# The third layer's sums over source nodes as pairs of float32r products

## What is computed

```python
h_edge = jnp.concatenate([x[src], x[dst]], axis=-1)
m_ij = jax.nn.relu(h_edge @ W_interact + b_interact)
m_i = jax.ops.segment_sum(m_ij, src, num_segments=x.shape[0])
m_i = m_i / jnp.asarray(math.sqrt(AVG_DEGREE), dtype=x.dtype)      # a factor 0.25
out = x + jax.nn.relu((x + m_i) @ W_update + b_update)
```

## Time and profile before

| | us |
|---|---|
| median of 3 runs (range) | 1886.35 (1883.08 to 1886.48) |
| span of the profiled execution, first to last instruction | 1885.1 |
| busy in that span: TensorE products, VectorE, ScalarE, GpSimd | 1694.0, 1432.5, 1037.5, 1024.9 |
| edge stage: first product of L1277 to last product of L1295, start to start | 1129.1 to 1877.2 |

### The profile page before, as it was taken

How to read it: one execution, slowest core, us unless ns; L and a number is a source line. 1 busy time by engine, 2 the same in 40 slices (tenths; PEclk the granted TensorE clock), 3 DMA queues, 4 the chain that set the end, 5 groups by cost and what they waited for, 6 DMA issues and landing times.

```text
span 1885.1 us, 45388 instructions
## 1 busy us (share of the span) xinstructions
PE 1694.0 (90%) x16778; PEld 1472.1 (78%) x16778; DVE 1432.5 (76%) x5527; ACT 1037.5 (55%) x2015; POOL 1024.9 (54%) x1075
## 2 busy tenths in 40 slices
PE   1606798999999979999999759999999999999998
PEld 1403676888778757777777649999999999999998
DVE  7968998999998335676653558888787777887776
ACT  1715575666667450000000248877777777777776
POOL 3364105656551004566551157777777777777775
PEclk9955999999999999999999879999999999999998
DMA  3005526465553656666666223443443444444442
GB/s 99 1 1 169 211 114 217 151 220 192 178 218 116 255 188 253 238 244 240 239 240 227 59 72 104 104 111 107 123 114 104 112 111 105 111 107 122 115 105 71
DMA packets 135014, 276.48 MB, mean 147 GB/s; under 512 B 21160, under 2 KB 82393, under 8 KB 134794
## 3 DMA queue, kind: packets, MB, share of 16 engines
q1 hardware_dynamic: 98427, 201.82, 31.1%
q0 software_dynamic: 34784, 71.17, 14.2%
q10 hardware_dynamic: 1584, 0.59, 0.1%
HBM read 192.26 MB, written 84.45 MB: 147 GB/s over the span
## 4 chain that ended last, share of the span: by engine, by line
PE 45%; DVE 24%; POOL 16%; issue 8%; DMA 4%; ACT 1%; POOLq 1%; SPq 1%; DVEq 0%
PE ps L1111 23%; POOL cells L810 8%; DVE hot L1595 7%; PE ps L1284 6%; PE ps L1277 5%; PE ps L1295 4%; POOL cell_lo L810 3%; POOL cell_hi L810 3%; DVE hot L1589 3%; PE ps L1097 2%; PE ps L1144 2%; DMA cells<-b_rows,work 2%; DVE keys L1685 1%; DVE keys L1619 1%; DVE keys L1684 1%
## 5 line engine op out<-in xcount | busy, mean ns | idle before, releaser
L1111 PE MATMUL ps<-slab,table 128*128 128x320 bf16 x4704 | 688.0, 300 | 2.5 <-DVE table L1834 2.4
L1111 PEld LDWEIGHTS ps<-slab,table 128*128 128x128 bf16 x4704 | 460.8, 98 | 167.9 <-DVE table L1834 2.9
L900 ACT ACTIVATE slab<-ps 128x980 bf16<-128x980 f32 x256 | 322.4, 1274 | 193.7 <-PE ps L1097 193.6
L810 POOL DMA_INDIRECT cells<-b_rows,work x336 | 319.9, 952 | 102.3 <-issue 96.9
L1284 PE MATMUL ps<-slab 125*128 125x128 bf16 x5496 | 357.1, 219 | 0.2 <-DVE slab L1917 0.2
L1284 PEld LDWEIGHTS ps<-slab 125*128 125x128 bf16 x5496 | 333.3, 98 | 4.8 <-DVE slab L1917 0.8
L1277 PE MATMUL ps<-table 125*128 125x128 f32 x1800 | 317.2, 286 | 1.7 <-DVE table L1911 1.7
L1005 ACT ACTIVATE lnw<-iota_w,keys 128x125 f32<-128x125 f32 x900 | 289.8, 389 | 1.6 <-POOL slab L801 1.6
L1277 PEld LDWEIGHTS ps<-table 125*128 125x128 f32 x1800 | 250.0, 192 | 1.9 <-issue 1.9
L1019 ACT ACTIVATE slab<-ps 128x384 f32<-128x384 f32 x300 | 146.1, 487 | 170.7 <-DVE ps L1926 167.6
L770 POOL DMA_INDIRECT hot<-t_rows,pairs x160 | 168.7, 1054 | 120.0 <-PE ps L1144 77.0
(11 more groups left out here) (304 smaller groups left out, 2144.6 us busy)
## 6 DMA issues: line engine op xcount, KB each, us to landing
slabs_d<-slab SPq DMA_DIRECT2D x16, 3920.0 KB, 12.9
slab<-slabs_d SPq DMA_DIRECT2D x16, 3920.0 KB, 14.4
hot<-lane_d SPq DMA_DIRECT2D x50, 576.0 KB
t_rows<-table SPq DMA_DIRECT2D x2, 4800.0 KB, 17.7
cells<-b_rows,work POOLq DMA_INDIRECT x336
inv<-inv_row SPq DMA_DIRECT2D x32, 160.0 KB
keys<-up_d SPq DMA_DIRECT2D x50, 96.0 KB
keys<-down_d SPq DMA_DIRECT2D x50, 96.0 KB
```

Source lines behind the costliest of these rows:

```text
L810: p.indirect_dma_start(rows_g[gi % RS][:, j, :], None, b_rows, bass.IndirectOffsetOnAxis(ap=node_t[:, t:t + 1], axis=0)).then_inc(e_gath[g ...
L900: a.activation(slab[par][:, :, u * UB * BW:(u + 1) * UB * BW].rearrange("p h (k d) -> p k h d", k=UB), psum_unit(u).rearrange("p k (h d) - ...
L1111: last = t.matmul(ps[:, 4 + par, 0:width], table[:, k // TERMS, k % TERMS, :], slab[par][:, k // TERMS, 0:width], start=k == 0, stop=k == ...
```

## The change

The messages are no longer one f32 tile. ScalarE writes relu(PSUM) rounded to type float32r (`msg_hi`), and a new VectorE instruction per group, `low_term`, writes the rest, max(PSUM, 0) - `msg_hi`, as float32r too (`msg_lo`, three buffers). The factor 0.25 goes into `src_hot`, which becomes float32r and 126 columns wide (BE). `source_sum` makes two float32r products for each tile in place of one f32 product: 1800 products in all. It now waits for `e_low`, and so does `edge_sum` for its bank; `low_term(gi - 1)` stands between `add_rows(gi)` and `prepare(gi + 3)`, and the last one behind the loop. A check is added: ahead of the loop two float32r products of 128x128 test tiles with VectorE making the tiles and comparing; behind the loop, VectorE looks at the lowest 12 bits of some of `msg_hi` (128x320), and adds 1e6 times what it found to the last chunk's rows, 128x640. The diff, without the places where semaphores are merged:

```diff
+    f32r = mybir.dt.float32r
...
+    BE = BN + 1
...
+        start = {}
+
+            start[name] = -(-nc.sbuf_base // 32) * 32
+
+        def over(name, of, byte, shape):
+            return nc.alloc_sbuf_tensor_at(name, shape, f32r, offset=start[of] + byte)
...
-        one_c = sb("one_c", [P, 1])
+        trial = over("trial", "pairs", 0, [P, 4, P])
+        quarter = sb("quarter", [P, 1])
...
-        msg_f = slab_f[0][:, NT * D:NT * D + 3 * GW]
-        assert NT * D + 3 * GW <= HI * SC // 2
-        msg = msg_f.rearrange("p (s n) -> p s n", s=3)
+        assert NT * D + 3 * GW <= HI * SC // 2 and (KU * FH + 2 * GW) * 4 + 24 <= 4 * 3 * KW // 2 and GW <= KW // 2
+        msg_hi = over("msg_hi", "slab0", 4 * NT * D, [P, 3, GW])
+        lo_two = over("lo_two", "work", -(-4 * KU * FH // 32) * 32, [P, 2, GW])
+        lo_one = over("lo_one", "iota_b", 0, [P, 1, GW])
+        msg_lo = [lo_two[:, 0, :], lo_two[:, 1, :], lo_one[:, 0, :]]
...
-        src_hot = [x[:, :, :].rearrange("p s n -> p (s n)")[:, k * GT * BN:(k + 1) * GT * BN].rearrange(
-            "p (j n) -> p j n", j=GT) for x in (tslot, rest) for k in range(3)]
+        src_hot_r = [over(f"src_hot_{of}", of, 0, [P, 3, GT * BE]) for of in ("tslot", "rest")]
+        src_hot = [x[:, k, :].rearrange("p (j n) -> p j n", j=GT) for x in src_hot_r for k in range(3)]
...
             def source_hot(gi):
                 if gi > 5:
                     act.wait_ge(e_psum, gi - 5)
-                far = lnw[:, :, :].rearrange("p k t -> p (k t)")[:, 0:GT * BN].rearrange("p (j n) -> p j n", j=GT)
+                far = lnw[:, :, :].rearrange("p k t -> p (k t)")[:, 0:GT * BE].rearrange("p (j n) -> p j n", j=GT)
                 if gi:
                     act.wait_ge(e_srchot, gi)
                 for j in range(GT):
-                    last = a.activation(far[:, j, :], iota_w[:, 0:BN], ACT.Square,
+                    last = a.activation(far[:, j, :], iota_w[:, 0:BE], ACT.Square,
                                         bias=lane_g[:, gi * GT + j:gi * GT + j + 1])
                 last.then_inc(e_far, 1)
                 act.wait_ge(e_far, gi + 1)
-                a.activation(src_hot[gi % 6], far, ACT.Relu, scale=-1.0, bias=one_c[:, 0:1]).then_inc(e_srchot, 1)
+                a.activation(src_hot[gi % 6], far, ACT.Relu, scale=-0.25, bias=quarter[:, 0:1]).then_inc(e_srchot, 1)
 
             act.wait_ge(q_lane, 1)
             act.wait_ge(f_blo, 6)
...
                 act.wait_ge(e_full, gi + 1)
                 if gi > 2:
                     act.wait_ge(e_psum, gi - 2)
-                a.activation(msg[:, gi % 3, :], ps[:, gi % 4, 0:GW], ACT.Relu, scale=0.25).then_inc(e_msg, 1)
+                a.activation(msg_hi[:, gi % 3, :], ps[:, gi % 4, 0:GW], ACT.Relu).then_inc(e_msg, 1)
                 if gi + SOON < NGR:
                     source_hot(gi + SOON)
 
...
                     t.matmul(ps[:, 6, 0:BN], g_msg, g_hot, start=True, stop=True).then_inc(g_sum, 1)
 
             pe.wait_ge(f_aok, NC)
+            pe.wait_ge(f_bok, NC)
             pe.wait_ge(f_blo, 6)
+            pe.wait_ge(s_trial, 2)
+            t.matmul(ps[:, 7, 2 * P:3 * P], trial[:, 0, :], trial[:, 1, :], start=True, stop=True)
+            t.matmul(ps[:, 7, 3 * P:4 * P], trial[:, 2, :], trial[:, 3, :], start=True, stop=True).then_inc(s_trial, 1)
 
             def edge_sum(gi):
                 b, g = divmod(gi, GB)
                 pe.wait_ge(e_rowhot, gi + 1)
                 if gi > 3:
-                    pe.wait_ge(e_msg, gi - 3)
+                    pe.wait_ge(e_low, gi - 3)
                 end = END_TILES[g]
                 w0, w1 = window(b, end)
                 for j in range(GT):
...
 
             def source_sum(gi):
                 b, g = divmod(gi, GB)
-                pe.wait_ge(e_msg, gi + 1)
+                pe.wait_ge(e_low, gi + 1)
                 pe.wait_ge(e_srchot, gi + 1)
                 if g == 0 and b > 1:
                     pe.wait_ge(e_added, b - 1)
+                terms = msg_hi[:, gi % 3, :], msg_lo[gi % 3]
                 for j in range(GT):
-                    last = t.matmul(ps[:, 4 + b % 2, 0:BN], msg[:, gi % 3, j * P:(j + 1) * P], src_hot[gi % 6][:, j, :],
-                                    start=g == 0 and j == 0, stop=g == GB - 1 and j == GT - 1)
+                    for k, term in enumerate(terms):
+                        last = t.matmul(ps[:, 4 + b % 2, 0:BE], term[:, j * P:(j + 1) * P], src_hot[gi % 6][:, j, :],
+                                        start=g == 0 and j == k == 0, stop=g == GB - 1 and j == GT - 1 and k == 1)
                 last.then_inc(e_psum, 1)
 
             def update(c):
...
 
             dve.wait_ge(f_aok, NC)
             dve.wait_ge(f_blo, 6)
+            link(v.tensor_scalar(trial[:, 0, :], ident[:, :], 1.0 + 2.0 ** -11, None, ALU.mult))
+            link(v.tensor_copy(trial[:, 2, :], ident[:, :]))
+            v.tensor_scalar(trial[:, 3, :], ones[:, :], 1.0 + 2.0 ** -11, None, ALU.mult).then_inc(s_trial, 1)
+            v.tensor_copy(trial[:, 1, :], ones[:, :]).then_inc(s_trial, 1)
 
             def prepare(gi):
                 b, g = divmod(gi, GB)
...
                 v.tensor_tensor(out=to, in0=to, in1=rows_g[gi % RS].rearrange("p j f -> p (j f)"), op=ALU.add
                                 ).then_inc(e_full, 1)
 
+            def low_term(gi):
+                dve.wait_ge(e_msg, gi + 1)
+                if gi > 2:
+                    dve.wait_ge(e_psum, gi - 2)
+                v.scalar_tensor_tensor(out=msg_lo[gi % 3], in0=ps[:, gi % 4, 0:GW], scalar=0.0,
+                                       in1=msg_hi[:, gi % 3, :].bitcast(f32), op0=ALU.max, op1=ALU.subtract
+                                       ).then_inc(e_low, 1)
+
             def keep_sum(b):
                 dve.wait_ge(e_psum, (b + 1) * GB)
                 to = hT[:, b * BN:(b + 1) * BN]
...
             AHEAD = 3
             for gi in range(AHEAD):
                 prepare(gi)
+            dve.wait_ge(s_trial, 3)
+            link(v.tensor_scalar(inv[:, 0, 0:2 * P], ps[:, 7, 2 * P:4 * P], 1.0 + 2.0 ** -11, None, ALU.not_equal))
+            v.tensor_reduce(out=col[:, 0:1], in_=inv[:, 0, 0:2 * P], op=ALU.max, axis=AX.X)
             for gi in range(NGR):
                 b, g = divmod(gi, GB)
                 add_rows(gi)
+                if gi:
+                    low_term(gi - 1)
                 if gi + AHEAD < NGR:
                     prepare(gi + AHEAD)
                 if g == AHEAD and b:
...
                     biased(LAST_BLOCK.index(b - 2))
                 if g == 2 and b - 2 in LAST_BLOCK:
                     residual(LAST_BLOCK.index(b - 2))
+            low_term(NGR - 1)
             keep_sum(NB - 1)
+            link(v.tensor_scalar(inv[:, 0, 0:SC].bitcast(i32), msg_hi[:, 0, 0:SC].bitcast(i32), 4095, None, ALU.bitwise_and))
+            link(v.tensor_copy(inv[:, 1, 0:SC], inv[:, 0, 0:SC].bitcast(i32)))
+            link(v.tensor_reduce(out=col[:, 1:2], in_=inv[:, 1, :], op=ALU.max, axis=AX.X))
+            link(v.tensor_tensor(out=col[:, 2:3], in0=col[:, 0:1], in1=col[:, 1:2], op=ALU.max))
+            link(v.tensor_scalar(col[:, 2:3], col[:, 2:3], 1.0e6, None, ALU.mult))
             biased(NC - 1)
+            dve.wait_ge(o_biased, NC)
+            link(v.tensor_scalar(hrow[:, (NC - 1) % 2, :, :], hrow[:, (NC - 1) % 2, :, :], col[:, 2:3], None, ALU.add))
             residual(NC - 1)
```

More of the change, by code:

```diff
@@ L322, in gnn_kernel @@
         s_diag = sem("s_diag")
-        s_et = sem("s_et")
+        s_once = sem("s_once")
         k_flag = sem("k_flag")
-        k_sum = sem("k_sum")
         s_rounds = sem("s_rounds")
@@ L334, in gnn_kernel @@
         k_placed = sem("k_placed")
+        ONCE_EDGES, ONCE_FLAGS, ONCE_BLOCKS, ONCE_ENDS = 1, 2, 3, 4
         def norm_sems(k):
@@ L414, in gnn_kernel @@
         e_msg = sem("e_msg")
+        e_low = sem("e_low")
+        s_trial = sem("s_trial")
         e_psum = sem("e_psum")
@@ L690, in _ @@
             numbers(up_c[:, :], [[BN, 12]], 1)
-            p.memset(one_c[:, :], 1.0).then_inc(s_iota, 1)
+            p.memset(quarter[:, :], 0.25).then_inc(s_iota, 1)
             p.iota(down_c[:, :], pattern=[[BN, 12]], base=BN - 1, channel_multiplier=-1,
@@ L1037, in _ @@
                 last = t.matmul(ps[:, 4, h * HG:(h + 1) * HG], ones[0:HG, :], diag[:, h, :], start=True, stop=True)
-            last.then_inc(s_et, 1)
+            last.then_inc(s_once, 1)
             def norm_transpose(S, c):
@@ L1063, in _ @@
             pe.wait_ge(k_flag, 2)
-            t.matmul(ps[:, 7, 0:1], ones[:, :], flag[:, 2:3], start=True, stop=True).then_inc(k_sum, 1)
+            t.matmul(ps[:, 7, 0:1], ones[:, :], flag[:, 2:3], start=True, stop=True).then_inc(s_once, 1)
             pe.wait_ge(s_w, 16 * 11)
@@ L1170, in spread_histogram @@
                 t.matmul(ps[:, 7, 0:HH * TH * HL - half], ones[0:TH * HH, :], flat[:, half:HH * TH * HL],
-                         start=True, stop=True).then_inc(q_need, 1)
```

(16 more changed lines are left out.)

3 lines of the change are left out of this document (removed).

## The result

The changed kernel is slightly slower: 1888.96 us (median of 20 runs, 1886.24 to 1893.34) against 1885.49 us for the kernel before (20 runs, 1883.08 to 1888.72), ratio 1.0022 with a 95% interval of 1.0016 to 1.0028, 3 to 5 us. That the change would gain nothing was foreseen. The extra time was not: I forecast 1.5 us more, at the end of the kernel, and the runs show 3 to 5 us, most of it in the gathers.

What follows compares the result with a forecast made beforehand. GpSimd's gathers were taken to bound the edge stage. Span 1885.1 + 0 (stage) + 1.5 (tail) = 1886.6 us; with the runs' median 1.25 above the profiled span, 1887.9 us, range 1880 to 1912.

Steps and rivals of the forecast that it cites:

- The bound: Edge stage: GpSimd's gathers set the pace at 2.50 us a group, 4% more than TensorE's 2.40.
- float32r at the price of a transpose: TensorE's source sums: each float32r product taken at 0.109 us, 196 us in place of 200, nothing gained.
- Rival 1: Source sums: a float32r product takes 0.222 us, as long as f32; TensorE sets the pace, about 2059 us; chance 0.16.
- the 715 us case: TensorE's sum of work in the stage if float32r counts as FP32 for weight loading; otherwise 620 us.
- The low term's price: VectorE, each group: 0.48 us plus 0.05 for two more waits, 0.53; demand 2.43 us a group, hidden by 0.07.
- The end: Tail from the last row sum: source sums +0.6 us and an uncovered 128x640 sum 0.88, together +1.5 us.
- the bare sum: Tail: the added wait and 128x640 sum ahead of `residual`, uncovered, 0.45 to 0.88 us, taken as 0.88.
- Stage: 0: Edge stage: no gather is touched and added work hides under the gathers, so the stage's time changes by 0.
- rival 3: Edge stage: VectorE's added work slows the gathers; +144 us if each low term blocks GpSimd for 0.48 us; chance 0.02.
- the 5.1 us over an even pitch: Gathers' time above 1.25 us each, listed as possible gain in the faster case, down to 1880; chance 0.05.
- the signs of being wrong: Profile signs: GpSimd waiting over 0.3 us for row sums, gathers' median leaving 944 ns, or a shorter stage with the same gathers.

Runs made afterwards that it cites:

- the unused term: Kernel before, f32 products kept, plus an unused VectorE instruction like the low term after each row sum: 1889.7 us against 1886.5, ratio 1.0021 without pauses.
- the earlier gathers: Kernel before with two subtractions moved from GpSimd to VectorE so gathers begin sooner: 1885.2 us against 1888.3, ratio 0.9990 without pauses.

## Why the prediction was right, and where it wasn't

**The bound.** Right. TensorE showed 99% busy and did not bind: 100 us less work gave a ratio of 1.0001. The view that told it was the gathers' line, not the busy shares. TensorE's own pace is 2.45 us a group, not my 2.40; the margin is half of what I computed.

**float32r at the price of a transpose.** Right: 0.111 to 0.118 us a product against the 0.109 taken, and TensorE is as busy in the stage as before. Rival 1 (0.222 us) is out. By the Trainium skill's rule ("TensorE: Matmul & The Clock Gate", "Weight-path perf modes — Fast Weight Load (FWL) and DoubleRow") this fits float32r counting as FP32 for the weight load, the 715 us case; that the load is what limits was not tried by itself.

**The low term's price.** Taken at 0.53 us, it is 0.47 from start to start, the rate of the row sum; the two more waits cost nothing. VectorE's demand is 2.35 us, not 2.43. Right side, more room.

**The end.** Mis-sized. +1.5 was forecast from the last row sum on; +0.1 was measured in the first profile (10.3 us against 10.2) and -0.7 in the second (9.5). The forecast took the middle between source sums at the full and at the half clock. On the changed kernel's timeline they go at the full one, 2.4 GHz: the granted clock is 1.00 until 1879.6, where before it had fallen to 0.50 (1.2 GHz) at 1875.5. TensorE had been busy without a break up to 1876.3 here, and before it stood idle for 1.2 us at 1872.6 and for 1.1 at 1874.8. The first row is from before, the second from after (order as in the earlier trace rows):

```profile
1876.00:1877.00 1.00, 1.00 (x5) 1.00 (x6) 0.00 (x0) 0.00 (x0) 0.00 (x0) 0.50 0.00 0
```

```profile
1877.00:1878.00 1.00, 0.76 (x7) 0.76 (x7) 0.74 (x2) 0.25 (x1) 0.00 (x0) 1.00 0.02 8
```

```profile
1876.64 0.55 DVE L1951 SCALAR_TENSOR_TENSOR lo_two<-ps,msg_hi 128x384 fp32r<-128x384 f32 x1
...
1877.29 0.56 DVE L1951 SCALAR_TENSOR_TENSOR lo_one<-ps,msg_hi 128x384 fp32r<-128x384 f32 x1
...
1879.17 2.12 PE L1322 MATMUL ps<-w_u,hT 128*128 128x128 f32 x10 [0.38 <-DVE hT L1958]
...
1881.43 0.82 DVE L1964 TENSOR_TENSOR hrow<-ps,bias 128x640 f32<-128x640 f32 x1 [0.81 <-PE ps L1322]
1882.29 0.55 DVE L2002 TENSOR_SCALAR hrow<-hrow,col 128x640 f32<-128x640 f32 x1
```

The two low terms' source sums end at 1878.8, 2.5 us after the last row sum, where one took 2.7 before. The update gains 0.4 (2.12 against 2.50), and the bare sum costs 0.59 with its wait, where 0.88 was taken. One piece was not forecast at all: from the last gather to the last row sum it is 3.2 us in both profiles of the changed kernel, and 2.5 to 2.7 before, with the unused term, without low terms and with the earlier gathers. Those 0.7 us are seen in the changed kernel alone; their cause is not shown.

**"Stage: 0".** This is the step that failed, by 3.3 us. I held the gathers' pace to be fixed, and weighed the opposite as rival 3, with 0.02, in a form that was too crude (every low term blocks GpSimd for its length, +144 us). The low term itself blocks nothing. Counted in the trace of the changed kernel, 160 gathers start while a low term runs, and none of them lasts over 15 ns more than the median. Of 49 that start while L1929 runs, 71% do, and the 49 last 80 ns longer on average (before: 54 gathers, 39%, 35 ns). Over 1.02 us last 18 gathers before, 32 and 27 in the two profiles after, 44 with the unused term and 15 without low terms. So the new instruction moves the others against the gathers.

How the move makes it worse can be counted too. Not every gather under L1929 (L1911 in the kernel before) is held, but mostly those that start 50 to 150 ns after it: they last 75 to 129 ns longer on average in the six profiles without pauses that this was counted in, the others under it 3 to 11 ns. There are 28 such gathers after (25 in the second profile) and 42 with the unused term, against 19 before, 19 without low terms and 11 with the earlier gathers. In the first profile they make 2.1 of the 2.6 us that the gathers last more beyond their median, and the meetings with `residual` (last section) make about 1 us, while the others got fewer. No other order of VectorE's work, without such meetings, was tried, so this is a count and not an experiment. Why only those 100 ns matter is not shown.

The rows of before had the sign. Beside the median of 944 ns stand maxima of 1241 and 1213, and the 5.1 us over an even pitch, which I listed as what could be gained, are the held gathers (5.8 us beyond their median). I read the median and went by it in rival 3 and in the signs of being wrong; it stayed at 945 to 947 while the time moved.

**Where the total ended.** The forecast's 1887.9 us and the measured 1888.96 are close in part by luck. The forecast stood on a median of three runs, 1886.35 us; over 20 runs the kernel before has 1885.49. So the step forecast is 1.5 us, and the step measured is 3.5 by the medians, 3 to 5 by the interval. The ratio of 1.0022 lies just outside the 0.2% that I had set for no change, the medians' difference just inside.

## What to carry to other kernels

Two engines at the same pace hide each other: look for the one that waits for nobody at an even pitch, whatever its busy share (GpSimd's was 76% against TensorE's 99%). Before a product is cut into cheaper passes, ask what one record of that form costs; here a record cost the same in both forms, and there were as many of them. And an instruction that fits into another engine's idle time can still cost, by where it pushes its neighbours: look at the longest of the bounding engine's instructions, not only at their median.

## What I had not expected of the hardware

A VectorE instruction with two SBUF operands can hold a gather for nearly its own length. In the changed kernel's timeline L1971 (`residual`, 128x640, both inputs in SBUF) and a gather start together:

```profile
1461.77 0.94 POOL L821 DMA_INDIRECT cells<-b_rows,work  x1 [0.30 <-issue]
...
1463.02 1.64 POOL L821 DMA_INDIRECT cells<-b_rows,work  x1 [0.30 <-issue]
1463.02 0.82 DVE L1971 SCALAR_TENSOR_TENSOR slab<-hrow,slab 128x640 f32<-128x640 f32 x1
```

The gather lasts 1.64 us in place of 0.94, 0.70 more, of the 0.82 that L1971 takes. There were three such in the changed kernel's profile, one before, and six of 1.50 to 1.71 us with the unused term. They follow one pattern: the gather ends 0.81 to 0.82 us after `residual` has ended. The same holds for shorter delays, as for two gathers in the kernel before that start 0.42 and 0.40 us after L1945 and last 1213 and 1241 ns. The Trainium skill ("SBUF — State Buffer", "SBUF: two separate sides") calls the ports that VectorE and GpSimd share an exclusive lock that is held for the whole instruction; this row agrees as to the length of the hold. By the same section of the Trainium skill whichever starts first gets the ports. Here the gather starts first, by 0.01 us, and is held all the same, as were seven of the nine gathers in six profiles that started up to 0.08 us before `residual`. I had cited that rule only for the instruction that was added, and not for those that it moves.

The other surprise is the pauses. With the same program, the kernel before took 1885 us at some times and 2160 to 2190 at others, with the gathers' own durations unchanged (median 944 ns in the changed kernel without its check) and their rows landing as soon as ever (2.5 us). It was TensorE that stood still, and both kernels with half the gathers, run beside those that paused, have none of it in the stage. At those times nothing that the experiments changed on VectorE or TensorE could be told from no change.
